# 64x64 transposes on TensorE: the transposing form for the blocks that land in rows 0 to 63

## What is computed

```
# layer 0: 16 heads, 64 key features, 128 value features, a state S of 64x128 for each head
S = a_t * (S - b_t * k_t (k_t . S)) + k_t v_t
o_t = S . q_t
# layer 1: 16 heads of 16 features, blocks of 64 tokens, causal inside the block
att = softmax(mask(q k^T / 4));  out = att v
```

## Time and profile before

| | |
|---|---|
| median of 3 runs | 7472.01 us (7466.28 to 7480.6) |
| the profiled execution | 7487.58 us |
| its span, first to last instruction | 7484.5 us |
| mean granted TensorE clock | 0.917 of full speed |
| TensorE matmuls busy | 6325.5 us, 85% of the span |
| TensorE weight loads busy | 4574.5 us, 61% |
| VectorE, ScalarE, GpSimd busy | 61%, 35%, 30% |

### The profile page before, as it was taken

One profiled execution on the slowest core, in us unless ns is written; L12 is line 12 of the kernel. 1 busy time (PEld: TensorE's weight loads), 2 busy tenths in 40 slices (PEclk: granted clock), 3 DMA queues, 4 the chain that ended last, 5 costly groups with the idle time before them and its releaser, 6 DMA issues. The chain is left out here.

```text
span 7484.5 us, 162627 instructions
## 1 busy us (share of the span) xinstructions
PE 6325.5 (85%) x60192; PEld 4574.5 (61%) x60192; DVE 4573.0 (61%) x9685; ACT 2618.9 (35%) x5275; POOL 2267.8 (30%) x3893
## 2 busy tenths in 40 slices
PE   7888888988889888888888888788888888888887
PEld 4665746656566665656657566565755657566575
DVE  6556675665756657565566656657556575655664
ACT  3334242332424325243242423324233252432421
POOL 2513224151331514215133241423315133151321
PEclk9899998999989999898988989899899998999998
DMA  1110001011010110001100010110101010011100
GB/s 53 33 38 22 27 31 38 29 28 34 21 36 29 32 41 22 23 29 32 41 22 27 31 36 31 22 40 21 35 29 32 30 33 23 29 32 41 22 27 5
DMA packets 376536, 226.37 MB, mean 30 GB/s; under 512 B 336896, under 2 KB 353920, under 8 KB 367488
## 3 DMA queue, kind: packets, MB, share of 16 engines
q1 hardware_dynamic: 375680, 215.29, 9.9%
HBM read 156.54 MB, written 58.72 MB: 29 GB/s over the span
## 5 line engine op out<-in xcount | busy, mean ns | idle before, releaser
L1580 PE MATMUL PS<-BIG 64*64 64x128 f32 (+3 forms) x23200 | 1094.5, 260 | 235.9 <-PEq L2026 105.5
L827 DVE SCALAR_TENSOR_TENSOR PS<-BIG,CW,PS 128x512 f32<-128x512 f32 x1536 | 1155.8, 753 | 215.6 <-DVEq L825 137.3
L1580 PEld LDWEIGHTS PS<-BIG 64*64 64x64 f32 (+2 forms) x23200 | 933.1, 138 | 379.9 <-issue 368.6
L1580 PE MATMUL PS<-XT,BIG 128*128 128x512 f32 x2048 | 1068.4, 655 | 50.1 <-PEq L1891 50.1
L1583 PE MATMUL PS<-CST,BIG 128*128 128x128 f32 x3536 | 558.5, 296 | 312.8 <-PEq L1658 82.8
L1583 PEld LDWEIGHTS PS<-CST,BIG 128*128 128x128 f32 x3536 | 415.8, 149 | 434.6 <-issue 417.8
L1243 POOL TENSOR_TENSOR FR<-MS,NHALF 128x8 f32<-128x8 f32 x128 | 209.9, 1640 | 1485.2 <-POOLq L1242 1303.7
L1580 PEld LDWEIGHTS PS<-XT,BIG 128*128 128x128 f32 x2048 | 400.7, 207 | 399.5 <-issue 390.3
L1089 POOL TENSOR_TENSOR RSTD<-VAR,NHALF 128x2 f32<-128x2 f32 x202 | 142.3, 704 | 1602.0 <-POOLq L1088 1595.3
L1580 PE MATMUL PS<-BIG,CST 128*128 128x256 f32 (+1 forms) x1360 | 507.8, 519 | 112.1 <-PEq L1961 98.9
L1171 POOL TENSOR_TENSOR BIG<-BIG 128x30 f32<-128x30 f32 (+14 forms) x960 | 499.9, 521 | 136.4
(11 more groups left out here) (152 smaller groups left out, 10194.1 us busy)
## 6 DMA issues: line engine op xcount, KB each, us to landing
BIG<-in_wv SPq DMA_DIRECT2D x16, 2048.0 KB, 7.4
BIG<-in_wo SPq DMA_DIRECT2D x16, 2048.0 KB, 8.7
BIG<-in_wq SPq DMA_DIRECT2D x16, 1024.0 KB, 4.9
BIG<-in_wk SPq DMA_DIRECT2D x16, 1024.0 KB, 7.6
cells_in<-BIG SPq DMA_DIRECT2D x128, 128.0 KB, 2.7
BIG<-cells_in SPq DMA_DIRECT2D x32, 512.0 KB, 3.7
cells_out<-BIG SPq DMA_DIRECT2D x32, 512.0 KB, 2.6
cells_nat<-BIG SPq DMA_DIRECT2D x32, 512.0 KB, 3.6
```

Of the source, the lines that this page charges most:

```text
L827: op = v.scalar_tensor_tensor(y, pre[:, j:j + G], CW[:, i * TAPS + j:i * TAPS + j + 1], y, ALU.mult, ALU.add)
L1580: return nc.tensor.matmul(out_, l, r, start=start, stop=stop)
```

## The change

Both places now call `turned`. Where the result goes to the lower rows (`to == 0`) it asks for the transposing form; where it goes to the upper rows it is the ordinary matmul, as before. Nothing else changes: the same blocks, in the same order, with the same waits and signals.

```diff
             def tr(out_, in_):
                 return nc.tensor.matmul(out_, in_, ident, is_transpose=True, start=True, stop=True)
 
+            def turned(out_, in_, lo, hi, to):
+
+                return nc.tensor.matmul(out_, in_, cst("ident_s")[lo:hi], is_transpose=to == 0, start=True, stop=True)
+
...
                             for lo, hi in halves:
-                                i = mm(ps[lo:hi, n * BLK:n * BLK + BLK], QKR[lo:hi, at:at + BLK], cst("ident_s")[lo:hi])
+                                i = turned(ps[lo:hi, n * BLK:n * BLK + BLK], QKR[lo:hi, at:at + BLK], lo, hi, lo)
...
                             for (lo, hi), (to, end) in zip(halves, across(m)):
-                                i = mm(cols(bank(2), m, C)[to:end], kq[lo:hi, m, 0, c * C:c * C + C], cst("ident_s")[lo:hi])
+                                i = turned(cols(bank(2), m, C)[to:end], kq[lo:hi, m, 0, c * C:c * C + C], lo, hi, to)
```

## The result

The change makes the kernel slower: 8069.35 us, median of 4 runs (8053.16 to 8085.37), against 7473.61 us for the kernel before in the same session. The ratio is 1.080, with an interval of 1.077 to 1.082. That is 596 us more, outside the forecast's range. The profiled execution's span is 8065.6 us.

The account below looks back on a forecast made before the run. The prediction took TensorE's work to bound the kernel nearly everywhere. Its sum, 1568 removed passes x 0 us, left the median at 7472 us, with a range of 7457 to 7487 us, and 7425 to 7568 us for 8 in 10.

Parts of the forecast that it names:

- What bounds the kernel: Whole kernel: TensorE's work bounds it nearly everywhere; 85% to all of a change in its time reaches the end.
- What the change removes: `keys_t` and the step of the tail: 1024 and 544 passes go, together 1568, and nothing else.
- Rival 1: Both places: both quarters share one pace, so removed passes save 39 to 46 us, 7426 to 7433 us; chance 0.20.
- The price of the transposing pass: Both places: a 64x64 transposing pass takes 0.0585 us, like an ordinary one.
- The step that failed: Both places: transposing and ordinary passes overlap in their quarters, so a pair stays at 0.117 us and the sum is 0.
- rival 3: Both places: each change of form changes the array's division and empties it, 318 to 374 us slower; chance 0.16.
- main case: Both places: the two forms run side by side, no change, 7457 to 7487 us; chance 0.45.
- Rival 2: Both places: the forms don't overlap but the array isn't emptied, 0.1755 us a pair, 78 to 92 us slower; chance 0.19.

Follow-up runs that it names:

- e5: Kernel before with its ordinary form, but the blocks for the lower rows left out at both places: 7473.27 us, ratio 0.9996.
- e1: Kernel of TensorE streams alone: T a 64x64 transpose in transposing form, N ordinary 64x64, W ordinary 64x128; T alone 0.056 us, T and N in turn 0.43 us.
- e4: Changed kernel with all transposing blocks (lower rows) of each place first, then all ordinary ones (upper rows): 7566.91 us, ratio 1.0122.

## Why the prediction was wrong

**What bounds the kernel** was right. TensorE's time went to the end for the most part: between the two profiled executions the span grew by 581 us and PE's busy time by 759, while no other engine moved. The difference of 178 us came out of TensorE's idle time, so 77% of the added busy time reached the end, less than the 85% to all that the prediction counted.

**What the change removes** was right, 1568 passes, and so was their worth. "The upper block is still there and still takes two passes, and the removed pass ran beside it" is what e5 shows, 0.9996. Rival 1, the shared pace, is out by the same run.

**The price of the transposing pass**, taken as 0.0585 us, was right: 0.056 in e1.

**The step that failed** is the condition at the end of the sum, "as long as the two forms run side by side". They don't: T and N in turn take 0.43 us whether or not they use different quarters, where the sum had 0.117 for the pair, and in the block of `keys_t` shown above no two passes start together. The argument against rival 3, that by their operands all blocks are 64x64 before and after, took the operands for the division of the array. The streams show that a 64x64 transpose goes without a gap beside 64x128 matmuls and with one beside 64x64 ones. The prediction priced this rival and gave it 0.16, though it quoted the rule of the Trainium skill that decides for it. No row spoke against the rule; the row on changing form without cost came from 128x128 matmuls, where the division is the same for both forms. That row was no evidence on 64x64 blocks.

**Rival 3 was the mechanism, and its size was 374 us at most; 596 was measured.** Three terms were short:

- Its pair was 0.117 + 2 x 0.09 + 0.0585 = 0.356 us, measured 0.43 (0.428 by the gaps 0.17, 0.11 and 0.15 of the block above, which are 0.172, 0.107 and 0.149 in the trace to the nanosecond). On the way from T to N the change costs 0.172 - 0.056 = 0.116 us, not 0.09. From N to T it is 0.149 - 0.058 = 0.09, as read from the earlier trace rows.
- The second ordinary pass starts 0.107 us after the first, not 0.0585. In e1's stream of N alone (line 40), which follows 128x128 matmuls, this happens once, at its start; here it comes after every change. With the larger first change it adds 0.07 us a pair. At the full clock the change thus costs 1568 x (0.428 - 0.117) = 488 us.
- The rest, 596 - 488 = 108 us, fits the clock. The prediction had left a lower clock "inside the main case", and for another reason, the fewer passes. Summed over the traces, the blocks of both places, each from its first to its last start, take 231 us before and 783 after, and 17 and 352 us of that are at the lower clock. A pair takes 0.64 us there instead of 0.43, so by an estimate 352 us hold 352 x (1 - 0.43 / 0.64) = 116 us of loss. It remains an estimate: no run held the clock up with the changes of division in place. In e4, with few such changes, the blocks spend 1 of 353 us at the lower clock.

**Rival 2** (no overlap, but no gap either, 0.1755 us a pair) isn't what the changed kernel does, but it is what e4 comes down to: 91 us measured, 78 to 92 priced. That the figures meet is in part luck: e4 still has a few changes of division, and its blocks last 121 us longer in the trace than those of the kernel before.

## What to carry over

A small float32 transpose in the transposing form takes the full width of the array for its rows, so it is cheap among 128-column work or among its own kind, and dear between 64x64 matmuls: each change of division cost 0.09 to 0.12 us in the changed kernel, more than the pass of 0.056 us between two of them. Before replacing instructions that run side by side, ask which quarter sets the pace; halving the passes of the other one gains nothing (e5). And a row that shows a change of form under one division of the array says nothing about the same change under another.

## What wasn't expected of the hardware

- The clock falls though PE is shown busy all the time, and gaps in the stream aren't the only way to it. In e1 the T and N stream began at 55.26 at the full clock and ran at half of it later. The stream of T and W in turn (66, 67), which has no gap at all, did the same: full from 204 to 208 us, half from 213 to 216, with PE and PEld both busy throughout. A stream of 256 transposes alone kept the full clock to its end, 14 us long. What tells these streams apart for the clock no run shows. Stretch, length, PE and PEld busy, POOL, PEclk:

```profile
61.00:69.00 8.00, 8.00 (x39) 5.14 (x38) 0.00 (x0) 0.50 0.01 2
...
204.00:208.00 4.00, 4.00 (x45) 4.00 (x45) 0.00 (x0) 1.00 0.00 0
213.00:216.00 3.00, 3.00 (x19) 3.00 (x18) 0.00 (x0) 0.50 0.00 0
...
316.20:330.70 14.50, 14.50 (x258) 14.39 (x257) 0.00 (x0) 1.00 0.01 2
```

- The page "TensorE: Matmul & The Clock Gate" of the Trainium skill, in its part on the PE-mode transpose, says of a 128x128 transpose in bf16 that the full clock doesn't engage in that mode. For the float32 transposes here the trace differs as far as it goes: a clock already full stayed full through 256 of them. Whether transposes alone would raise it from the lower level no run here shows.
- Two small transposes from different row halves, both with results in the lower rows, overlap fully (0.028 us each). A way to use that in this kernel, where half of the results have to go to the upper rows, wasn't tried.
